# Five sets of cross-attention key and value blocks instead of three, two slots of transposed probabilities instead of three, and the order of the work planned anew

## The reference

```
m = silu(cond) @ w_ada + b_ada                 # 9 vectors of 256 for each sequence
h = ln(x)*(1+sc1)+sh1 ; x += g1 * (self_attention(h) @ w_so + b_so)     # 16 heads of 16, window 128
h = ln(x)*(1+sc2)+sh2 ; q = h@w_q ; k,v = ctx@w_kv
    scores = q k / 4 ; keep the 16 largest of each row ; softmax over them ; x += g2*(o @ w_co + b_co)
h = ln(x)*(1+sc3)+sh3 ; x += g3 * ((silu(h@w_m1a) * (h@w_m1b)) @ w_m2 + b_m2)
# second layer: plain cross attention, context normalised, both sides scaled and shifted by silu(cond) @ Wss
x = x + softmax(q k / 4) v @ Wp + bp
```

## Time and profile before

| what | value |
|---|---|
| median of 3 runs | 647.51 us (647.25 to 649.8) |
| the profiled execution, whole time | 646.2 us |
| its span, first to last instruction | 644.1 us |
| PE busy | 611.9 us (95%), 6029 matmul instructions |
| DVE busy | 539.8 us (84%) |
| ACT busy | 495.0 us (77%) |
| POOL busy | 366.1 us (57%) |
| transfers | 32.21 MB, most of it in the first 50 us |

### The profile page before, as it was taken

The page is one execution under the profiler, slowest core; times in us unless marked ns, Lnnn a source line. Parts: engine busy times, 40 slices in busy tenths (PEclk is TensorE's granted clock), DMA queues, the critical chain, the costliest instruction groups (busy, mean ns, idle before and its releaser), DMA issues.

```text
span 644.1 us, 18326 instructions
## 1 busy us (share of the span) xinstructions
PE 611.9 (95%) x6029; PEld 526.9 (82%) x6029; DVE 539.8 (84%) x2281; ACT 495.0 (77%) x1907; POOL 366.1 (57%) x625
## 2 busy tenths in 40 slices
PE   6887999999999999999999999999999999989897
PEld 5676979788898989888898979888898978877785
DVE  2688898979899898989899998989899897969342
ACT  1765588788888888797888878788897888866265
POOL 3446564747567573855657484637647384646430
DMA  7870010120110101220102201010101100010000
GB/s 241 288 312 26 1 43 2 43 82 3 40 54 2 51 17 51 60 66 2 51 2 72 62 3 66 29 41 2 66 10 36 42 2 27 2 50 2 34 1 18
DMA packets 20540, 32.21 MB, mean 50 GB/s; under 512 B 2464, under 2 KB 11808, under 8 KB 20192
## 3 DMA queue, kind: packets, MB, share of 16 engines
q1 hardware_dynamic: 20448, 31.05, 14.9%
HBM read 28.85 MB, written 2.20 MB: 48 GB/s over the span
## 4 chain that ended last, share of the span: by engine, by line
PE 61%; DVE 19%; ACT 9%; POOL 5%; issue 3%; DMA 2%; SPq 1%; DVEq 0%; POOLq 0%; ACTq 0%
PE ring L1242 11%; PE ring L1081 10%; PE ring L1075 9%; PE ring L1199 8%; PE ring L1250 7%; PE s_bank L1186 6%; ACT probs L824 6%; PE ring L1219 5%; DVE left L989 3%; DVE left L1002 3%; DVE top L978 3%; PE ring L1133 2%; DVE top L996 2%; DVE neg_max L970 2%; POOL left L763 2%
## 5 line engine op out<-in xcount | busy, mean ns | idle before, releaser
L824 ACT ACTIVATE probs<-s_bank,neg_max 128x128 f32<-128x128 f32 x512 | 180.6, 404 | 8.3 <-DVE neg_max L970 7.3
L831 ACT ACTIVATE probs_t<-ring 128x512 f32<-128x512 f32 x192 | 112.5, 635 | 33.1 <-PE ring L1199 32.5
L824 ACT ACTIVATION_READ_ACCUMULATOR probs<-s_bank,neg_max 128x1 f32 x512 | 125.5, 245 | 0.0
L1242 PE MATMUL ring<-h_t,w_m 128*128 128x128 f32 x1024 | 123.3, 276 | 0.9 <-ACT probs_t L831 0.4
L1242 PEld LDWEIGHTS ring<-h_t,w_m 128*128 128x128 f32 x1024 | 118.2, 192 | 3.4 <-issue 2.5
L794 ACT ACTIVATE h_t<-ring,mod_all 128x128 f32<-128x128 f32 x160 | 64.9, 482 | 41.6 <-PE ring L1133 33.5
L821 ACT ACTIVATE probs<-s_bank,neg_max 128x128 f32<-128x128 f32 x256 | 75.4, 420 | 18.8 <-DVE left L989 18.8
L763 POOL TENSOR_TENSOR left<-left,probs 128x512 f32<-128x512 f32 x64 | 82.4, 1288 | 9.5
L970 DVE TENSOR_REDUCE neg_max<-s_bank 128x8 f32<-128x1024 f32 x64 | 76.9, 1210 | 9.1 <-PE s_bank L1186 8.9
L777 POOL TENSOR_TENSOR mlp<-mlp 128x512 f32<-128x512 f32 x32 | 40.7, 1272 | 66.8 <-ACT mlp L853 63.1
L1199 PE MATMUL ring<-ident,probs 128*128 128x128 f32 x512 | 70.6, 275 | 3.4 <-ACT mlp L853 0.7
(11 more groups left out here) (129 smaller groups left out, 1286.5 us busy)
## 6 DMA issues: line engine op xcount, KB each, us to landing
gates<-rows_dram SPq DMA_DIRECT2D x48, 256.0 KB, 3.7
x_res<-in_x SPq DMA_DIRECT2D x16, 128.0 KB, 3.7
ctx_in<-in_ctx SPq DMA_DIRECT2D x16, 128.0 KB, 3.3
ctx_t<-in_ctx_t SPq DMA_DIRECT2D x16, 128.0 KB, 3.1
w_m<-in_w_m SPq DMA_DIRECT2D x1, 2048.0 KB, 13.1
out_y<-x_res SPq DMA_DIRECT2D x16, 128.0 KB, 1.7
mlp<-in_w_ada SPq DMA_DIRECT2D x2, 512.0 KB, 6.7
w_m<-in_w_m SPq DMA_DIRECT2D x1, 1024.0 KB, 8.9
```

The source lines that it names most:

```text
L824: e = nc.scalar.activation(probs[:, k, u, j], s_bank[:, u, P * j:P * j + P], ACT.Exp, bias=neg_max[:, k, n:n + 1], accum_out=row_sum[:, k, ...
L831: nc.scalar.activation(dst, bank("T", which, b)[:], ACT.Relu if k == CROSS else ACT.Copy).then_inc(pt_ready, 1)
L1242: e = nc.tensor.matmul(d[:, P * j:P * j + P], w_m1[:, c, at:at + P], h_t[:, MLP, c], start=(c == 0), stop=(c == CK - 1))
```

## The change

Two constants change. The cross attention gets five sets of key and value blocks where it had three, and probs_t gets two slots where it had three. The one edit takes as much memory as the other gives: two sets of blocks are 8 KB in each partition (2 KB of keys and 2 KB of values each), and so is the third slot of probs_t. With two slots of probs_t, the step that loads the first weights uses slot 1 as before (`flat_pt[:, 1, ...]`).

With the constants, all five tables are new. They hold the same steps, the same number of each. The rest of the program is the same word for word, three lines further down.

```diff
-SLOTS = {SELF: 2, CROSS: 3, LAST: 3}
-TURNED = 3
+SLOTS = {SELF: 2, CROSS: 5, LAST: 3}
+TURNED = 2
...
-    ("load", "v", (446,)), ("load", "qk", (493,)), ("load", "x1", (540,)), ("load", "ctx0", (587,)),
-    ("store_rows", SELF, (937,)), ("load", "co", (982,)), ("load", "ada1g", (1029,)), ("load", "x2", (1076,)),
+    ("load", "qk", (446,)), ("load", "ada1g", (493,)), ("load", "x1", (540,)), ("load", "ctx0", (587,)),
+    ("load", "co", (634,)), ("load", "ada2g", (681,)), ("load", "v", (728,)), ("load", "x2", (775,)),
...
```

More of the change, by code:

```diff
@@ L46 @@
[L46 to L52, removed]
@@ L78 @@
[L78 to L85, removed]
@@ L102 @@
[L102 to L109, removed]
+    ("norm", SELF, (773, 1640, 2600, 4056, 6938, 10687, 13778, 14195,
+     21453, 24292, 28347, 30854, 35735, 38678, 42296, 46585)),
@@ L139 @@
[L139 to L142, removed]
-    ("exp", (CROSS, 0), (4124, 7824, 11064, 14863, 18483, 21838, 25379, 29341,
-     32928, 36181, 40125, 43488, 47023, 50871, 53949, 57399)),
-    ("exp", (CROSS, 1), (4382, 8005, 11458, 15166, 18736, 22270, 25871, 29498,
-     33177, 36727, 40274, 43864, 47500, 51096, 54282, 57857)),
@@ new lines @@
+    ("rows", MLP, (1941,)),
+    ("max", (SELF, 1), (2056, 3204, 6393, 9099, 12667, 16205, 20021, 23569,
+     27149, 30697, 34286, 37861, 41456, 45142, 48930, 52321)),
+    ("keys", CROSS, (2166, 5703, 6503, 10061, 13756, 17109, 21036, 24819,
+     28191, 31916, 35199, 38984, 42783, 46387, 49743, 53373)),
+    ("keys", LAST, (2246, 5499, 6583, 13665, 17516, 20570, 24535, 28271,
+     31836, 35425, 38868, 42454, 46024, 49823, 53582, 56664)),
+    ("inv", SELF, (2520, 3806, 6883, 10530, 14115, 17607, 21247, 24090,
+     28012, 32161, 35177, 39064, 42714, 46530, 49987, 53136)),
@@ new lines @@
+    ("mods", CTX, (1113,)), ("mod_turn", CTX, (1229,)),
+    ("qk", 0, (1244, 2120, 3174, 6077, 9476, 13080, 16654, 20097,
+     23914, 27562, 31120, 34738, 38321, 41918, 45416, 49051)),
+    ("rows", CROSS, (1426,)),
+    ("scores", SELF, (1601, 2637, 5446, 8647, 12172, 15675, 19410, 23087,
+     26644, 30267, 33856, 37337, 41010, 44646, 48272, 51897)),
+    ("turn", CTX, (1711, 4375, 5925, 12943, 16436, 19945, 24096, 27423,
[3 rows of a table added]
+    ("rows", MLP, (1825,)),
+    ("keys", LAST, (1940, 5223, 6374, 13422, 17087, 20458, 24372, 28085,
+     31463, 35261, 38664, 42261, 45912, 49540, 53134, 56430)),
@@ new lines @@
+    ("mods", LAST, (3659,)),
+    ("scores", CROSS, (3736, 6973, 10515, 14147, 17765, 21433, 25006, 28653,
+     32182, 35829, 39383, 43015, 46598, 50285, 53771, 57196)),
+    ("warm", 8, (3846,)),
+    ("values", LAST, (3981, 4670, 7083, 14890, 17632, 22255, 25907, 29396,
+     32860, 36615, 40397, 43810, 47410, 51207, 54792, 57578)),
+    ("warm", 10, (4114,)), ("warm", 17, (4491,)), ("warm", 12, (4758,)),
+    ("T", (CROSS, 0), (4875, 8446, 12045, 15630, 19528, 22997, 26577, 30142,
+     33764, 37472, 40965, 44601, 48187, 51774, 55404, 58368)),
@@ new lines @@
+    ("sums", CROSS, (5820, 9128, 12635, 16306, 19840, 23566, 27117, 30772,
+     34387, 37973, 41570, 45110, 48745, 52382, 55870, 59324)),
+    ("out", CROSS, (5989, 9297, 12855, 16475, 20009, 23735, 27335, 30941,
+     34556, 38142, 41739, 45328, 48963, 52551, 56039, 59493)),
+    ("turn", MLP, (6464, 9793, 13397, 16972, 20548, 24256, 27879, 31413,
[9 rows of a table added]
+    ("warm", 13, (7847,)),
+    ("down", MLP, (8072, 11485, 15151, 18826, 22412, 26098, 29662, 33285,
+     36794, 40485, 44122, 47708, 51319, 54949, 58472, 61155)),
```

611 lines of the change are left out of this document (304 added, 307 removed), and 37 rows, old and new, of tables (ACT_PLAN, DVE_PLAN, PE_PLAN).

## The result

The changed kernel takes 658.33 us (median of 4 runs, 657.86 to 659.86) where the kernel before takes 647.38 beside it: ratio 1.017 [1.0149, 1.0191], slower by 11 us. I had forecast 647.0 us, with 650.9 as the upper end of the range. The profiled execution has a span of 656.0 us, 11.9 more than before's 644.1.

A forecast was written before the change was run, and what follows sets the result against it. PE was taken to bound the middle, dependent chains both ends, with no clock term. Terms 0 - 0.7 - 1.0 + 0.5 + 0.6 + 0.4 - 0.3 = -0.5 us gave a median of 647.0 us, range 644.2 to 650.9.

The forecast's parts named there:

- Rival C: Start: CROSS scores wait for in_w_ss_q behind a late store, 6.1 us late, 653.1 us; chance of over 0.5% slower 0.11.
- Step 1: Start up to the first CROSS scores: they begin between 38.4 and 40.3 us, -0.7 to +1.2, taken as 0.
- step 7: End: a warm ahead of the last down is gone, other steps exchanged beside waits; gain 0.3, ends -0.9 and +0.9.
- Step 2: Masks of the first sequence: an addition goes behind the fourth mask; gain 0.7, bounds 0 to 1.7.
- Step 3: Load of context block 4, issued some 40 us earlier, ends DVE's idle near 140 us; gain 0 to 2.0, taken as 1.0.
- Step 4: Load of context block 10 becomes tight on DVE near 317 us; cost 0.5, up to 2.0.
- Step 5: One more warm step in the full middle, between SELF scores 4 and LAST scores 1; cost 0 to 0.9, taken as 0.6.
- Step 6: Lost probs_t slot: at 7 places sums move ahead of T and may wait for ACT; 0 to 2.1 us, taken as 0.4.
- The slots: CROSS keys and values: two sets alive before and after, so the added sets are not needed; price 0.
- A: Whole kernel: the order is better than seen, everything at its good end, together -5.3, 642.2 us; chance 0.09.
- B: Middle: more room was missing, so the 7.4 us of PE idle there would go, 640.1 us; chance 0.04.
- D: Many small waits in the middle, 653.8 us at worst, 650 at half; chance of over 0.5% slower 0.05.

The follow-up runs named there:

- e1: Changed kernel with one POOL step, norm of SELF for sequence 7, put back behind the masks and norm of MLP for sequence 3: 651.43 us, ratio 1.0070.
- e16: e15 with turn of SELF block 3 on PE directly behind v of block 2, its shift on ACT behind that v's copy: 645.32 us, ratio 0.9967.
- e9: Kernel before with two of the change's moves alone: skip of CROSS block 0 behind its fourth mask, load of ctx block 2 issued sooner: 647.82 us, ratio 0.9999.
- e4: Kernel before with norm of SELF for sequence 7 moved on POOL to directly ahead of the second glu of sequence 2: 652.59 us, ratio 1.0076.
- e7: Kernel before with the two new constants (five CROSS slots, two of probs_t) and nine moves of sums or T: 652.88 us, ratio 1.0096.
- e12: Kernel before with the nine moves of e7 alone, keeping its own constants (three CROSS slots, three of probs_t): 653.24 us, ratio 1.0088.
- e8: Changed kernel with e1's norm put back and two sets of CROSS keys and values in place of five: 651.19 us, ratio 1.0046.
- e5: e1 with the 1 MB load of w_m2 moved behind ctx_in, x4, in_w_ss_q, l_q and x3 on SP: 649.20 us, ratio 1.0021.
- e2: Changed kernel with the load of x for sequence 4 moved ahead of w_m2 on SP: 657.77 us, ratio 1.0170.
- e10: Changed kernel with the edits of e5 and e6 together: 647.75 us, ratio 1.0008.
- e6: e1 with x of sequence 4 loaded ahead of w_m2, and mods of LAST and its mod_rows moved behind the first CROSS scores: 650.66 us, ratio 1.0055.
- e11: e10 with scores of SELF block 2 on PE moved directly behind the second T of CROSS 0: 649.74 us, ratio 1.0025.
- e14: e15 with turn and shift of SELF block 3 moved earlier; it makes V of SELF block 2 from block 3's rows, a different computation: 645.90 us, ratio 0.9984.
- e15: e10 with norm of SELF block 3 and skip of SELF block 1 moved ahead of norm of CTX block 2 on POOL: 646.63 us, ratio 1.0003.

## Why the prediction was wrong, step by step

**Rival C was the mechanism of the first place, and I gave it 0.11.** Step 1 took 0 for the start of the CROSS scores (38.4 to 40.3 us, -0.7 to +1.2); they began at 42.71, +3.6. What failed in it is the landing of the store: I let it land at about 30 by bytes queued over the rate of the stretch, and it let SP go on at 33.55. The row of the same kind of store in the kernel before, 6.9 us, would have said 33.5; the measured wait was 6.2, the one for the SELF rows 8.6. I used that row for the rival and a rate for the forecast. in_w_ss_q was then issued at 36.13, 1.7 before rival C's 37.8, and the scores began at 42.71, 2.5 before its 45.2. Two more things were not in the sum. The x rows of sequence 4 stand behind the same store, with `q` of CROSS queued behind their `stats` on DVE. And the clock, which I wrote off with "no clock term", fell behind the wait: the scores alone took 0.94 us longer (2.09 against 1.15). The one profile that I had was of an execution at 1.00 throughout. Of the 90 executions of the kernel before that ran beside e1 to e16, 52 have a mean clock below 1.000.

**The second place was in no step and no rival.** The first part says that in the middle only idle PE time can be won or `warm` steps can cost, and step 7 calls the other changes steps exchanged beside waits. That sentence is the error of 5.8 us, and the clock term that was put at nothing has a part in it as well: of the 6.7 us that e1 takes away here, 5.25 are PE's wait and 1.45 are `down` at the lower clock. `norm` of SELF waits for the turn of the block before (line 737 of the changed kernel), and moving it 3,400 positions forward on POOL put both `glu` of sequence 2 behind that wait. I had asked of each step what it waits for on PE, and not, for every step moved on POOL, what is queued behind it there.

**Step 2** (masks, -0.7): wrong. The last mask ended 21.5 us after the CROSS scores (64.22 against 42.71), before 21.35; e9 shows no gain either. **Step 3** (context block 4, -1.0): the idle went, but e9's trace keeps 0.2 of it, and the changed kernel has +0.46 from C1 to C3. Even e9's first 1.07 us may not all be the edit's: e4, which left this load in its place, had 71.42. What is late next in e9 is the `inv` of CROSS 3 on DVE (167.29 us): POOL waits 0.84 us for it, and PE 0.58 us for POOL. **Step 4** (context block 10, +0.5): after the change DVE waits for ctx_in once in the whole kernel, 0.6 us; nothing shows at that place. **Step 5** (`warm`, +0.6): right in kind. The scores of LAST 1 lag by 0.95 us more than those of SELF 4 ahead of it, the size of one `warm`; 1.3 us come back by C3. **Step 6** (+0.4): no cost here. The waits of `sums` for ACT after the change:

```profile
PE ring L1222 <- ACT probs_t L834: 1.3, 3, 0.6
```

e7 and e12 show that the same tightening laid on the old order costs 5.5 to 6.1 us. The new order has another place for ACT's steps too, which may be how it avoids this; no run shows it. **Step 7** (end, -0.3): from the scores of CROSS 15 to the end it is +0.6. **The slots**: right, as e8 shows. Rivals A, B and D did not happen; D had small waits in many places where there was one of 5.3. **The range** has a slip of its own: its bounds, -1.9 and +3.1, are deviations from the sum and were laid around the old time. Around the forecast of 647.0 they give 645.1 to 650.1, and the result lies outside either.

The Trainium skill (DMA: Bandwidth & Descriptors, Queues, rings and completion order) was cited for rival C: descriptors of a queue are taken in ring order. The trace agrees: the store took 6.2 us with the 1 MB ahead of it and 4.8 in e5 without. It is not all of such a wait: the 6.9 us of the row in the kernel before, which the prediction counts as agreement, had no load of 1 MB ahead of it, only smaller ones.

## What to carry to other kernels

For a step that is moved on an in-order engine, write down what it waits for at its new place and what is queued behind it there; a step that nobody needs yet, put ahead of one that is needed now, costs the whole difference, and the lower clock behind the wait on top (5.6 to 6.9 us here for one norm). A wait for the landing of a small store is priced by the row of the same store under the same load, not by bytes over bandwidth. And when one late transfer is cured and nothing is gained, look for what else stands behind the same wait: e2 alone would have acquitted the transfers.

## What was not expected of the hardware

A store of 32 KB, where SP waited for it, took between 3.7 us (e10) and 9.2 us (e16) to come back, while the weights were being loaded (287 GB/s over 15 to 30 us of the changed kernel). After 3.4 us in which PE had nothing the granted clock was 0.53 over the next 5.4 us, and 16 small matmuls took 2.09 us instead of 1.15; a wait of 5.25 us in the middle of a full stretch was followed by 0.73 over 5.4 us, and one of 3.0 us in e4 by 0.68 over 5.3 us. e10 and e6 kept a lower clock (0.80 and 0.81 over 41.6:47) although PE's waits ahead of the scores were 1.1 and 0.5 us long. The rows do not settle what decides it: over 36.00 to 41.60 PE was busy 3.87 us in e10 at 0.88 and 3.34 us in e16 at 1.00, and in e16 the clock fell later, to 0.87 over 47 to 60 us:

```profile
36.00:41.60 5.60, 3.34 (x34) 2.83 (x35) 1.98 (x7) 2.26 (x12) 1.44 (x4) 1.00 0.98 324
```

Nor is it the order alone. e10, e11, e14, e15 and e16 have the same order up to the first CROSS scores. From 36 to 47 us the clock was below 1.00 in e10 and e15, from 47 to 60 us in e11 and e16, and in e14 in neither. It goes with the time of the whole: of the 90 executions of the kernel before, the 38 with a mean clock of 1.000 took 646.3 us on average, the 11 with 0.992 took 649.1. A single profile at 1.00, such as the one that the prediction was made from, shows nothing of this.
